# A transformer block with experts on one core: first expert tile turned by TensorE, and the order of roots and fills in the combination

## What is computed

```python
_, idx = jax.lax.top_k(logits + expert_bias, TOP_K)      # 2 of 8 experts
g_topk = jax.nn.softmax(sel, axis=-1)
for e in range(Wg.shape[0]):
    gate = jax.nn.silu(h @ Wg[e].T)
    up = h @ Wu[e].T
    oe = rmsnorm(gate * up @ Wd[e].T, enorm_w[e])
    out = out + gates[:, e:e + 1] * oe
s_hat = rmsnorm(out, out_norm_w) @ W_out.T
...
x = x + gb * _L0_ffn_ref(h, ...)
```

## Time and profile before

| | us |
|---|---|
| median of 3 runs | 411.15 |
| lowest and highest | 406.92 and 411.74 |
| the profiled execution | 410.28 |
| its span | 408.40 |
| mean granted PE clock (1 is 2.4 GHz) | 0.970 |
| PE busy in the span | 377.1 (92%) |

### The profile page before, as it was taken

One profiled execution on the slowest core, in us unless ns is written; L12 is line 12 of the kernel. 1 busy time (PEld: TensorE's weight loads), 2 busy tenths in 40 slices (PEclk: granted clock), 3 DMA queues, 4 the chain that ended last, 5 costly groups with the idle time before them and its releaser, 6 DMA issues.

```text
span 408.4 us, 13090 instructions
## 1 busy us (share of the span) xinstructions
PE 377.1 (92%) x3868; PEld 317.9 (78%) x3869; DVE 323.8 (79%) x1039; ACT 291.8 (71%) x815; POOL 239.9 (59%) x211
## 2 busy tenths in 40 slices
PE   7899998999999999998779999999999999999574
PEld 4688886888888888874369989999989899974453
DVE  5368998899999999886949878787878787862686
ACT  5455767887878888656438887878778778773685
POOL 0665587688888888866443554545554545554241
PEclk9599999999999999999989999999999999999689
DMA  7999863646464340011142333233332233214833
GB/s 219 359 366 399 298 226 117 222 133 220 138 211 151 129 129 26 28 53 40 50 56 47 74 59 71 59 71 62 68 69 61 58 71 74 44 41 134 333 89 93
DMA packets 47652, 52.60 MB, mean 129 GB/s; under 512 B 35203, under 2 KB 40982, under 8 KB 44790
## 3 DMA queue, kind: packets, MB, share of 16 engines
q1 hardware_dynamic: 43078, 42.84, 35.0%
q0 software_dynamic: 4544, 9.39, 7.3%
HBM read 35.60 MB, written 30.38 MB: 162 GB/s over the span
## 4 chain that ended last, share of the span: by engine, by line
PE 59%; DVE 17%; issue 8%; DMA 6%; ACT 6%; POOL 3%; DVEq 1%; SPq 0%; ACTq 0%; POOLq 0%
PE bank L1753 9%; PE bank L1754 8%; PE bank L1755 8%; PE bank L1484 7%; PE bank L1770 4%; PE bank L1772 4%; PE bank L1771 4%; DVE prod L965 4%; PE bank L1564 3%; PE bank L1507 2%; POOL dispatched L540 2%; DMA late<-expert_rows 2%; DVE wmaxs L1062 1%; DMA dispatched<-filler 1%; ACT junk L841 1%
## 5 line engine op out<-in xcount | busy, mean ns | idle before, releaser
L563 POOL DMA_INDIRECT expert_rows<-late,to_place x74 | 78.1, 1056 | 78.4 <-DVE late L1337 66.4
L1753 PE MATMUL bank<-late,w_hi 128*128 128x256 f16 x312 | 85.8, 275 | 4.2 <-DMA late<-dispatched 2.9
L522 POOL TENSOR_TENSOR kv<-kv,v 128x1024 f32<-128x1024 f32 x32 | 67.8, 2137 | 31.2 <-ACT kv L696 31.0
L1754 PE MATMUL bank<-late,w_hi 128*128 128x256 f16 x312 | 85.8, 275 | 0.0
L1755 PE MATMUL bank<-late,w_lo 128*128 128x256 f16 x312 | 85.7, 275 | 0.0
L540 POOL DMA_INDIRECT dispatched<-rows,pos x64 | 67.8, 1059 | 24.9 <-issue 18.5
L1323 DVE SCALAR_TENSOR_TENSOR kv<-bank,uscale,kv 128x512 f32<-128x512 f32 x78 | 58.4, 750 | 29.0 <-ACT kv L775 20.0
L1484 PE MATMUL bank<-cst,kv 128*128 128x128 f32 x576 | 73.8, 279 | 1.0 <-DVE den L1103 1.0
L775 ACT ACTIVATE kv<-bank,descale 128x512 f32<-128x512 f32 x78 | 53.5, 687 | 25.7 <-PE bank L1755 22.2
L1484 PEld LDWEIGHTS bank<-cst,kv 128*128 128x128 f32 x576 | 68.6, 193 | 1.7 <-issue 1.5
L781 ACT ACTIVATE kv<-kv 128x512 f16<-128x512 f32 x78 | 48.8, 625 | 16.0 <-DVE kv L1323 9.3
(11 more groups left out here) (243 smaller groups left out, 781.8 us busy)
## 6 DMA issues: line engine op xcount, KB each, us to landing
dispatched<-filler SPq DMA_DIRECT2D x17, 1032.0 KB
late<-wguT SPq DMA_DIRECT2D x1, 4096.0 KB, 18.3
late<-expert_rows SPq DMA_DIRECT2D x1, 2064.0 KB, 12.6
gates_bc<-gate_rows SPq DMA_DIRECT2D x1, 2048.0 KB, 7.5
wd<-wdT SPq DMA_DIRECT2D x1, 2048.0 KB, 25.3
out<-kv SPq DMA_DIRECT2D x16, 128.0 KB, 1.8
expert_rows<-late,to_place POOLq DMA_INDIRECT x78
late<-expert_rows SPq DMA_DIRECT2D x1, 1032.0 KB, 8.2
```

Source lines behind the costliest of these rows:

```text
L522: nc.gpsimd.tensor_tensor(kvt[:, 0:HD, :, :], k_in, v_in.to_broadcast([P, HD, H, HD]), ALU.mult).then_inc(kv_done[t], 1)
L563: pool.indirect_dma_start(ybuf, bass.IndirectOffsetOnAxis(ap=to_place[:, s, r:r + 1], axis=0), yt[:, s, r, :], None).then_inc(y_scat[s], 16)
L1753: mm(o, wh, hi, start=True, stop=False)
L1754: mm(o, wh, lo, start=False, stop=False)
```

## The change

It has three parts.

1. Tile 0's rows are loaded by a plain transfer, tokens on partitions, into the half of `rows` that belongs to even batches, whose scatters are over by then. PE turns the four 128x128 pieces (two halves, two blocks of tokens) by matmuls against a float16 identity into two PSUM banks, ACT copies the high and then the low halves into `hT3[:, 0]`, and the matmuls of tile 0 wait for these copies. The identity is one more cast on DVE among the constants. There are nine fills in front instead of eight.

2. On ACT the roots of the fourth load (g = 3) stand behind batch 1 instead of batch 2. On DVE its coefficients stand behind the mixing of batch 3 and the output of batch 1 instead of in front of them.

3. On PE there are 50 fills in front of the combination instead of 46, and seven, three and three new ones behind the projections of batches 0, 1 and 2, into a PSUM bank that the combination doesn't use.

```diff
+        ident16 = sb("ident16", [P, P], F16)
...
+        first_rows = rows[:, 0, :, 0, 0:D]
...
+        FIRST = [CUM[1 - half][:, 0:R] for half in range(2)]
...
                 if again_turn(i):
                     sp.wait_ge(u3_ps, 2 * t - 6)
+                elif s == 0:
+
+                    sp.dma_start(first_rows, hbuf[bass.ds(row, R), 0:D].rearrange(
+                        "(r p) w -> p r w", p=P)).then_inc(slot_ld[s], 16)
+                    return
                 sp.dma_start(hT3[:, s], hbuf16[bass.ds(row, R), 0:2 * D], transpose=True).then_inc(slot_ld[s], 16)
...
+            for half in range(2):
+                act.wait_ge(turn_ps, B + 4 + half)
+                nc.scalar.activation(hT3[:, 0, half], FIRST[half],
+                                     ACT.Copy).then_inc(hT_done, 1)
...
-                if b in (0, 2, 5):
-                    rms_of_rows((0, 2, 5).index(b) + 2)
+                if b in (0, 1, 5):
+                    rms_of_rows((0, 1, 5).index(b) + 2)
...
+            nc.vector.tensor_copy(ident16[:], ident)
...
             turn_of_batches(0, (2,))
+            turn_of_batches(0, (3,))
             coefficients(3)
-            turn_of_batches(0, (3,))
...
+                first_tile = isinstance(t, int) and t == 0
...
+                    if first_tile:
+                        pe.wait_ge(hT_done, B + 1)
                     mm(o, wh, hi, start=True, stop=False)
+                    if first_tile:
+                        pe.wait_ge(hT_done, B + 2)
                     mm(o, wh, lo, start=False, stop=False)
...
-            keep_busy(CUM[0], 8)
+            keep_busy(CUM[0], 9)
+
+
+            pe.wait_ge(slot_ld[0], 16)
+            for half in range(2):
+                for r in range(RB):
+                    last = mm(FIRST[half][:, r * P:(r + 1) * P], rows16[:, 0, r, 0, half * D:(half + 1) * D], ident16[:],
+                              start=True, stop=True)
+                last.then_inc(turn_ps, 1)
...
-            keep_busy(CUM[0], 46)
+            keep_busy(CUM[0], 50)
...
-            turn_of_batches(0, range(1, 4))
+            for j, n in ((1, 7), (2, 3), (3, 3)):
+                turn_of_batches(0, (j,))
+                keep_busy(ND, n)
```

## The result

| | before | after |
|---|---|---|
| median, us (20 runs each) | 410.99 | 407.43 |
| lowest to highest | 406.38 to 415.81 | 405.52 to 411.38 |
| the profiled execution, its span | 410.28, 408.40 | 408.94, 407.10 |
| mean granted PE clock in it | 0.970 | 0.979 |

The ratio of the runs is 0.9939, with a 95% interval of 0.9917 to 0.9960: a gain of 2.5 us (1.6 to 3.4). The medians alone are 3.6 us apart.

What follows compares the result with a forecast made beforehand. PE was taken to bound the expert stage (busy 39.65 of 40 us); in the combination, its clock fallen, PE needs as much per batch as ACT and DVE. Sum: 410.28 - 2.9 - 1.7 = 405.7 us, range 402.7 to 408.6.

Steps and rivals of the forecast that it cites:

- The mechanism of part 1: Start of experts: plain load lands in 2.1 us, first matmul near 205.3, second tile near 208.1, clock staying up.
- The term of 2.9 us: Start of experts: second tile's first matmul at 208.0 or 208.1 instead of 210.96, a gain of 2.9 us.
- the 1.35 of earlier data: Start of experts: share of the 2.9 us gain from tile 0's data being ready earlier, 206.85 against 205.5.
- the 1.55 of the clock: Start of experts: share of the 2.9 us gain from PE's clock not falling to 1.2 GHz.
- Rival B: Start of experts: plain load lands no sooner than the transposing one, second tile 0.6 us late; 409.2 us, chance 0.07.
- Parts 2 and 3: Combination: reordered roots and coefficients plus added fills gain 1.7 us, bounds 0.3 and 2.5.
- Rival C: Before experts and in combination: fills at the low clock stand in the way, costing 0.8 and 1.0; 412.1 us, chance 0.05.
- Rival D: Combination stays bound by its loads, so parts 2 and 3 give only 0.3 us; 407.1 us, chance 0.08.
- Rival A: Start of experts: the clock falls all the same, leaving only 1.35 of the first gain; 407.2 us, chance 0.10.
- I add nothing: Whole time: no term for the three-run median 0.87 above the profiled run or one run 4.2 below; both kept in range.

Runs made afterwards that it cites:

- fills alone: The kernel before with only the 4 + 7 + 3 + 3 combination fills added, roots' order as before; ratio 0.9996 (0.9958 to 1.0035).
- roots alone: The kernel before with only the fourth load's roots and coefficients reordered, 46 fills and no more; ratio 0.9990 (0.9952 to 1.0028).
- hold and combination: The kernel before with the second transposing load issued only when the first has landed, plus parts 2 and 3; ratio 0.9976 (0.9928 to 1.0024).
- the fourth set: Against before on one chip: changed kernel with 62 instead of 50 fills, 0.9980; changed kernel, 0.9937; part 1 alone, 0.9967.

## Why the prediction was right and wrong

- *The mechanism of part 1* was right step by step: plain load 2.21 us (2.1 taken), first matmul 3.28 behind the fills' start (3.2), second tile 5.91 (5.9 to 6.0), no fall of the clock. The gate's table load stood in the way by as much as was said and cost nothing; the second transposing load was in time.
- *The term of 2.9 us was mis-sized, and this is the step that failed*: "whose rows were there shortly before 206.85, some 4.6 us after its issue" was read off one execution and taken for the load's price. In nine executions with that load unchanged, the second tile starts between 5.57 and 9.04 us behind the fills; in five of them at 5.6 to 5.7, which is 0.3 *earlier* than with part 1. With the 16 KB packet less than 1 us behind the issue it is 6.56 with the transposing load and 6.85 with the plain one, again 0.3 earlier: so what part 1 gains on the mean may be that the packet fell beside its load less often (once in seven, against four in nine), and not the plain load; no run separates the two. Both halves of the term hang on it, the 1.35 of earlier data and the 1.55 of the clock, since the clock fell only where PE had waited 2.5 us or more. The mean gain of this part is 0.94 on the chips at 411 us, a third of the term.
- *Rival B* had the warning in hand: rows 7 showed 2.6 to 3.3 us for the landings of the same kind of load, and the forecast held against B the 1.8 of the plain one. In the early executions the transposing load's rows were used 2.98 us after its issue (203.37 to 206.35), the plain one's 2.21 after its own. The transposing one is slower, so B's mechanism isn't what happened, but by 0.8, which turn and copies eat; only the price of B (0.6 late) was near the truth there (0.3 late).
- *The rule of the Trainium skill* (Advanced Engine Details and Errata, section X-Bar Transpose (TRN2)), that transposing DMAs are as fast as regular ones, isn't borne out to the letter (2.98 against 2.21 us for these 128 KB), but it was the better guide to the size than the 4.6 us of the one trace.
- *Parts 2 and 3*: 1.7 was forecast, and 1.45 came in the profiled pair, 1.88 over the traces on such chips. Batch 8's squares, of which 1.7 was said, came 1.32 us nearer to the end of the experts. Beside the traces of its own chip, fills alone (34.93) gives 1.0 us against 35.95 on the mean of three, and roots alone (35.08) 0.3 against one, 35.42; with both, where the clock held, it is 34.0, but on other chips. That the two parts add up isn't shown. Batch 3 was taken without idle, batch 4 was mixed at 384.89 + 0.94 = 385.83 (385.75 said). The roots started at 381.82 behind the fourth load (382.1 said) and the squares of batch 2 at 382.17 (382.42).
- *Rival C* (fills at a low clock stand in the way) didn't come in the measured pair and did on another chip, from the side that I hadn't named: not a fall at the first turn in spite of the fills, but fills that had run out before the last scatters landed. Its price was as much as the gain, so no change, not a loss. It is one trace of the changed kernel and one of hold and combination.
- *Rival D* didn't come in the measured pair: the loads landed in time. In the changed kernel's trace of the fourth set the third load cost 0.56 us. *Rival A* didn't either; in all seven traces with part 1 the clock stayed up at the start.
- *"I add nothing"* for the difference between executions was the second error. The attention stage alone moves by 3.2 us (202.08 to 205.28) between executions on the chips at 411 us, 1.66 of it with a fall of the clock at 73 us that comes and goes; a forecast against a single profiled execution inherits its luck at every such place.

## What to carry to other kernels

Before a wait of one trace is made a term of a sum, ask whether it repeats: look for the same instruction elsewhere in the trace, and take the range of its landings, not the one value that the change would remove. Where a load varies so, ask also which other queues moved packets in the same microseconds. A wait behind which the clock falls costs twice, once by itself and once by the slow matmuls behind it, so an execution in which it was long shows a gain that most executions don't have to give. Fills are a bridge of fixed length over a wait of varying length: 50 of them left PE at most 0.4 us of idle on the chips at 411 us and 2.81 on a slower one, and twelve more delayed batch 1 by 1.1 us where the wait was short. Part of them behind the event that ends the wait, as in front of the experts, would vary less with it; that wasn't tried here.

## What the runs showed that I had not expected

- The same transposing load of 256 rows of 512 B, the first of three, let PE start 2.95, 3.0, 3.9, 4.4 or 4.8 us behind fills that started 0.06 us before its issue. In the four latest of the nine, and in no other, a 16 KB packet of the queue for instructions lay within 3 us behind the issue. Holding the second load back didn't make the first come sooner than it also comes without.
- Chips differ by 2 to 3% with the same program (411 against 420 to 422 us); in the traces the fills in front of the experts start at 209.7 to 215.4 us against 202.1 to 205.3, and the five loads are issued 6.4 to 8.3 us behind the first fill of the combination against 5.5 to 6.3. Why wasn't looked into.
- Nine runs of a kernel that differs from before by one cast that nothing reads gave 0.9928 with an interval that excludes 1; twelve more on another chip gave 0.9994.
